# A local-attention stage with 64-key bands computed as 64x32-tile products, and value copies made by DMA

## The reference, cut to what matters

```
bk2, bv2 = (look(bk), look(bv))          # a window's own 32 keys and the 32 before
mask = (it < jb) | (it > jb + w) | (jb == -1)
sim = jnp.einsum('bhwie,bhwje->bhwij', bq, bk2) * QK_SCALE
sim = jnp.where(mask, -jnp.finfo(sim.dtype).max, sim)
attn = jax.nn.softmax(sim, -1)
out = jnp.einsum('bhwij,bhwje->bhwie', attn, bv2)
```

## Time and profile before

| | us |
|---|---|
| median of 3 runs | 2713.26 |
| lowest, highest | 2708.19, 2714.23 |
| span of the profiled execution | 2713.2 |
| one pass of the steady loop (8 slots), profiled | 38.97 to 38.99 |

### The profile page before, as it was taken

One profiled execution on the slowest core, in us unless ns is written; L12 is line 12 of the kernel. 1 busy time (PEld: TensorE's weight loads), 2 busy tenths in 40 slices (PEclk: granted clock), 3 DMA queues, 4 the chain that ended last, 5 costly groups with the idle time before them and its releaser, 6 DMA issues.

```text
span 2713.2 us, 62249 instructions
## 1 busy us (share of the span) xinstructions
PE 2525.8 (93%) x18693; PEld 2059.1 (76%) x18693; DVE 2253.2 (83%) x5097; ACT 1560.3 (58%) x3463; POOL 1737.4 (64%) x1485
## 2 busy tenths in 40 slices
PE   6999799989999899999999998999989999899998
PEld 4774577768887688886788867888768888688886
DVE  4778788878998699996899978999778989699995
ACT  3545455656665466664666655666546666466663
POOL 3444311168886487884788747887657888388883
PEclk9998899989999999999999999999999999999999
DMA  3000000100000100000000001000010000000000
GB/s 86 0 0 0 1 0 0 40 25 0 0 0 4 38 1 0 0 0 17 25 0 0 0 8 34 0 0 0 8 33 0 0 0 0 17 1 0 0 0 16
DMA packets 27720, 24.09 MB, mean 9 GB/s; under 512 B 11734, under 2 KB 24164, under 8 KB 26852
## 3 DMA queue, kind: packets, MB, share of 16 engines
q1 hardware_dynamic: 27620, 22.96, 2.9%
HBM read 21.90 MB, written 1.05 MB: 8 GB/s over the span
## 4 chain that ended last, share of the span: by engine, by line
PE 57%; DVE 17%; issue 8%; ACT 4%; DVEq 1%; POOL 1%; ACTq 0%; POOLq 0%
PE bank L688 10%; PE bank L728 7%; PE bank L754 6%; PE bank L715 5%; PE bank L493 5%; DVE l_ss L1434 4%; DVE xs_part L1411 4%; PE bank L701 4%; DVE l_rot L1424 4%; ACT l_sq L1032 3%; PE bank L742 3%; PE bank L693 3%; PE bank L645 2%; PE bank L710 2%; PE bank L634 1%
## 5 line engine op out<-in xcount | busy, mean ns | idle before, releaser
L443 POOL TENSOR_TENSOR l_rn<-l_ss,minus_half 128x8 f32<-128x8 f32 x384 | 632.3, 1647 | 192.6 <-DVE l_ss L1444 171.7
L441 POOL TENSOR_TENSOR l_qk<-l_rot 128x512 f32<-128x512 f32 x384 | 488.1, 1271 | 164.5 <-DVE l_rot L1424 162.0
L447 POOL TENSOR_TENSOR l_qk<-l_qk,l_rn 128x512 f32<-128x512 f32 x384 | 400.5, 1043 | 55.0
L1037 ACT ACTIVATE l_qkT<-bank 128x512 f32<-128x512 f32 x384 | 229.4, 597 | 334.2 <-PE bank L701 334.1
L1032 ACT ACTIVATE l_sq<-bank 128x512 f32<-128x512 f32 x384 | 229.9, 599 | 312.1 <-PE bank L688 302.5
L728 PE MATMUL bank<-l_v,probT 128*128 128x65 f32 x3072 | 389.4, 270 | 9.0 <-ACT probT L893 8.9
L728 PEld LDWEIGHTS bank<-l_v,probT 128*128 128x128 f32 x3072 | 374.8, 192 | 13.3 <-ACT probT L893 12.6
L1420 DVE TENSOR_TENSOR l_rot<-bank,l_tab 128x512 f32<-128x512 f32 x384 | 264.1, 688 | 139.6 <-ACT l_sq L1032 139.4
L1132 DVE TENSOR_REDUCE peak<-bank 128x4 f32<-128x512 f32 (+1 forms) x512 | 348.3, 680 | 36.8 <-PE bank L531 30.3
L688 PE MATMUL bank<-w_high,xs_part 128*128 128x512 f32 x768 | 341.7, 445 | 33.8 <-DVE xs_part L1411 33.8
L888 ACT ACTIVATE prob<-sm 128x512 f32<-128x512 f32 x512 | 319.1, 623 | 83.5 <-DVE sm L1140 77.3
(11 more groups left out here) (187 smaller groups left out, 4761.7 us busy)
## 6 DMA issues: line engine op xcount, KB each, us to landing
early<-in_L_ffn_Wqkv_dram SPq DMA_DIRECT2D x6, 1536.0 KB, 6.6
l_wo<-in_L_ffn_Wo_dram SPq DMA_DIRECT2D x6, 512.0 KB, 3.6
f_w<-in_L_ffn_W_dram SPq DMA_DIRECT2D x6, 341.0 KB
out_dram<-X SPq DMA_DIRECT2D x4, 256.0 KB, 2.3
f_w<-in_L_ffn_W_dram SPq DMA_DIRECT2D x6, 128.0 KB
l_oT<-in_L_xattn_Wkv_dram SPq DMA_DIRECT2D x1, 512.0 KB, 5.7
const<-in_const_dram SPq DMA_DIRECT2D x1, 392.0 KB, 3.1
f_b<-in_L_ffn_b_dram SPq DMA_DIRECT2D x24, 0.5 KB
```

Of the source, the lines that this page charges most:

```text
L441: pool.tensor_tensor(l_qk[:, k], l_rot[:, k, 0], l_rot[:, k, 1], ALU.add).then_inc(l["add_done"], 1)
L443: pool.tensor_tensor(l_rn[:, k], l_ss[:, k], minus_half[:], ALU.pow).then_inc(l["rn_done"], 1)
L447: pool.tensor_tensor(v, v, l_rn[:, k, :, None].broadcast_to([128, 8, L_DIM]), ALU.mult).then_inc(l["qk_done"], 1)
```

## The change

Every 32 queries meet the 64 keys of their band only. Scores are 16 products for a unit (2 head pairs, 4 windows, 2 halves of the rows) of 64 rows, 32 columns of queries and 64 keys, instead of four over 128 keys; the mask (l_mask) is 128 columns wide instead of 256. Peaks, subtraction, exponential and the copy of the turned probabilities take 256 columns instead of 512, and two transposes take the place of four. A turned block then holds the band keys of one head in partitions 0 to 63 and of another in 64 to 127. The products with the values are 16 of 64 rows and 32 columns, and need the values at matching partitions: besides l_v, two arrangements l_v2 (moved by 32 keys) and l_v3 (halves exchanged), which four DMAs for each batch fill on SP (move_values). They share room with buffers of the first stage (stash). PE waits for them once in a batch (moved).

The result of l_pv stands in banks 6 and 5, columns 256 on. Bank 5 also takes the turned probabilities, so l_turn waits for o_done, the divide of the unit before. The lists of stages are in another order on PE, ACT and DVE:

```diff
+BAND = 2 * WINDOW
+WINDOWS = S // WINDOW
...
+        l_mask = sb("l_mask", [128, 2 * BAND], BF16)
...
-        a_km = sb("a_km", [128, 2, 4, 128])
+        stash = sb("stash", [128, 2 * 2 * 4 * 2 * (L_DIM + 1)])
+        a_km = stash[:, 0:1024].rearrange("p (k h n) -> p k h n", k=2, h=4)
+        l_v2, l_v3 = (stash[:, 1040 * k:1040 * (k + 1)].rearrange("p (b u r n) -> p b u r n", b=2, u=4, r=2)
+                      for k in range(2))
+        a_q, a_k, a_o, a_oT = (stash[:, 1040 + 256 * k:1296 + 256 * k].rearrange("p (k n) -> p k n", k=2)
+                               for k in range(4))
...
-        l_v = sb("l_v", [128, UNROLL, 4, L_DIM + 1])
+        l_v = sb("l_v", [128, 2, 2, 4, 2, L_DIM + 1])
...
+            def move_values(ub, b, k):
+                sp.wait_ge(l["v_done"], upto(ub, 4 * b + 4))
+                apart(sp)
+                if not isinstance(b, int) or b >= 2:
+                    sp.wait_ge(l["pv_done"], upto(ub, 4 * b - 4))
+                    apart(sp)
+                for dst, half, at in ((l_v2, 0, 32), (l_v2, 1, 32), (l_v3, 0, 64), (l_v3, 1, 0)):
+                    sp.dma_start(dst[64 * half:64 * half + 64, k], l_v[at:at + 64, k, half]).then_inc(moved, 16)
+            def serve_layer(ly, last):
+                ub = ly * UNITS
+                if not last:
+                    sp.wait_ge(l["w_split"], upto(0, (ly + 1) * W_CHUNKS))
+                    apart(sp)
+                    load_projections(ly + 1)
+                for b in range(2):
+                    move_values(ub, b, b)
+                with sp.Fori(1, B // 2) as i:
+                    for k in range(2):
+                        move_values(ub, 2 * i + k, k)
+                if not last:
+                    sp.wait_ge(l["out_done"], upto(0, (ly + 1) * B))
+                    apart(sp)
+                    load_output(ly + 1)
...
+                def l_turn(u, b, j):
+                    pe.wait_ge(l["exp_done"], upto(ub, u + 1))
+                    pe.wait_ge(l["probT_done"], upto(ub, u))
+                    pe.wait_ge(l["o_done"], upto(ub, u))
+                    for r in range(2):
+                        ins = pe.transpose(bank[:, 5, r * 128:(r + 1) * 128], prob[:, j % 2, r * 128:(r + 1) * 128],
+                                           ident)
+                    ins.then_inc(l["turned"], 1)
...
-                        pe.matmul(bank[:, 3 + r, 0:256], ident_bf, mask_bf, start=True, stop=False,
+                        pe.matmul(bank[:, 3 + r, 0:2 * BAND], ident_bf, l_mask[:], start=True, stop=False,
                                   skip_group_check=True)
                     for p in range(2):
-                        for r in range(2):
-                            rows = slice(64 * r, 64 * r + 64)
-                            ins = pe.matmul(bank[:, 3 + r, 128 * p:128 * p + 128],
-                                            l_qkT[rows, j % 2, 128 * p:128 * p + 128],
-                                            l_qkT[rows, j % 2, 256 + 128 * p:384 + 128 * p],
-                                            start=False, stop=True, skip_group_check=True)
+                        for w in range(WINDOWS):
+                            keys = 256 + 128 * p + max(w - 1, 0) * WINDOW
+                            queries = 128 * p + w * WINDOW
+                            for r in range(2):
+                                rows = slice(64 * r, 64 * r + 64)
+                                ins = pe.matmul(bank[w * WINDOW:(w + 1) * WINDOW, 3 + r, BAND * p:BAND * (p + 1)],
+                                                l_qkT[rows, j % 2, queries:queries + WINDOW],
+                                                l_qkT[rows, j % 2, keys:keys + BAND],
+                                                start=False, stop=True, skip_group_check=True)
...
                 def l_pv(u, b, j):
                     pe.wait_ge(l["probT_done"], upto(ub, u + 1))
-                    pe.wait_ge(l["v_done"], upto(ub, u + 1))
                     pe.wait_ge(l["o_done"], upto(ub, u))
-                    w = L_DIM + 1
-                    for h in range(4):
-                        n = h % 2 * 2 + h // 2
-                        ins = pe.matmul(bank[:, 6, h * w:(h + 1) * w], probT[:, j % 2, n * 128:(n + 1) * 128],
-                                        l_v[:, j, h, :], start=True, stop=True)
+                    if j % 4 == 0:
+                        pe.wait_ge(moved, (ly * B + b + 1) * 64)
+                    apart(pe)
+                    k, g = j // 4, j % 4
+                    values = ((l_v[:, k, 0], l_v[:, k, 0], l_v2[:, k], l_v3[:, k]),
+                              (l_v3[:, k], l_v3[:, k], l_v2[:, k], l_v[:, k, 1]))
+                    for r in range(2):
+                        for w in range(WINDOWS):
+                            for p in range(2):
+                                rows = slice(64 * p, 64 * p + 64)
+                                at = 256 + (L_DIM + 1) * r
+                                ins = pe.matmul(bank[w * WINDOW:(w + 1) * WINDOW, 6 - p, at:at + L_DIM + 1],
+                                                probT[rows, j % 2, 128 * r + w * WINDOW:128 * r + (w + 1) * WINDOW],
+                                                values[p][w][rows, g, r], start=True, stop=True,
+                                                skip_group_check=True)
                     ins.then_inc(l["pv_done"], 1)
...
-                return Pipeline(pe, [(6, lambda u, b, j: turn(l, ub, u, j)), (4, l_scores), (7, l_turn_o), (6, l_pv),
-                                     (3, l_turn_qk), (7, l_output), (0, l_turn_x), (1, l_project)],
-                                UNITS, UNROLL, 4)
+                return Pipeline(pe, [(6, l_turn), (1, l_project), (4, l_scores), (6, l_pv), (3, l_turn_qk),
+                                     (7, l_turn_o), (7, l_output), (0, l_turn_x)], UNITS, UNROLL, 4)
...
+                def l_exp(u, b, j):
+                    act.wait_ge(l["sub_done"], upto(ub, u + 1))
+                    act.wait_ge(l["turned"], upto(ub, u - 1))
+                    act.activation(prob[:, j % 2, 0:4 * BAND], sm[:, j % 2, 0:4 * BAND], ACT.Exp, scale=QK_SCALE)\
+                       .then_inc(l["exp_done"], 1)
+                def l_copy_prob(u, b, j):
+                    act.wait_ge(l["turned"], upto(ub, u + 1))
+                    act.wait_ge(l["pv_done"], upto(ub, u - 1))
+                    act.activation(probT[:, j % 2, 0:256], bank[:, 5, 0:256], ACT.Copy).then_inc(l["probT_done"], 1)
...
-                    act.activation(l_v[:, j, :, 0:L_DIM],
-                                   bank[:, 1, 0:256].rearrange("p (h n) -> p h n", n=L_DIM), ACT.Copy)\
+                    act.activation(l_v[:, j // 4, :, j % 4, :, 0:L_DIM],
+                                   bank[:, 1, 0:256].rearrange("p (h r n) -> p h r n", h=2, r=2), ACT.Copy)\
                        .then_inc(l["v_done"], 1)
...
-                return Pipeline(act, [(6, lambda u, b, j: copy_prob(l, ub, u, j)), (1, l_copy_x),
-                                      (5, lambda u, b, j: exp(l, ub, u, j, QK_SCALE)), (7, l_copy_o), (3, l_copy_qk),
-                                      (1, l_square), (1, l_copy_v)], UNITS, UNROLL, 4)
+                return Pipeline(act, [(6, l_copy_prob), (1, l_copy_x), (5, l_exp), (1, l_square), (1, l_copy_v),
+                                      (3, l_copy_qk), (7, l_copy_o)], UNITS, UNROLL, 4)
...
                 def l_divide(u, b, j):
+                    ov = bank[:, 5:7, 256:256 + 2 * (L_DIM + 1)].rearrange("p a (r n) -> p a r n", r=2)
+                    sums = rsum[:, j % 2, 0:4].rearrange("p (a r) -> p a r", a=2)
                     dve.wait_ge(l["o_turned"], upto(ub, u - 1))
-                    invert_sums(l, ub, u, j, 4, L_DIM)
-                    divide(l, ub, u, j, 4, L_DIM, o[:, j % 2].rearrange("p (h n) -> p h n", n=L_DIM))
+                    dve.wait_ge(l["pv_done"], upto(ub, u + 1))
+                    dve.reciprocal(sums, ov[:, :, :, L_DIM]).then_inc(l["rsum_done"], 1)
+                    dve.wait_ge(l["rsum_done"], upto(ub, u + 1))
+                    dve.tensor_tensor(o[:, j % 2].rearrange("p (a r n) -> p a r n", a=2, r=2)[:, ::-1],
+                                      ov[:, :, :, 0:L_DIM],
+                                      sums[:, :, :, None].broadcast_to([128, 2, 2, L_DIM]), ALU.mult)\
+                       .then_inc(l["o_done"], 1)
...
-                return Pipeline(dve, [(0, l_copy_in), (1, l_split_x), (4, l_peaks), (2, l_floor), (4, l_shift), (6, l_divide),
-                                      (7, l_residual), (1, l_rotate), (1, l_sum_squares)], UNITS, UNROLL, 4)
+                return Pipeline(dve, [(0, l_copy_in), (1, l_split_x), (2, l_floor), (1, l_rotate), (4, l_peaks),
+                                      (4, l_shift), (1, l_sum_squares), (6, l_divide), (7, l_residual)],
+                                UNITS, UNROLL, 4)
...
```

66 lines of the change are left out of this document (40 added, 26 removed).

## The result

The changed kernel takes 3192.64 us (median; 3187.24 to 3210.04), the kernel before 2713.74 beside it: 1.177 times the time before, with an interval from 1.174 to 1.181. The forecast was 3149, with a range from 3015 to 3330.

A forecast was written before the change was run, and what follows sets the result against it. It took a circle through PE, ACT and DVE to bound the changed kernel: batch 24.32 us, 4.83 over 19.49, +406 in 84 batches; 2713 + 406 + 30 outside the loops = 3149 us, range 3015 to 3330.

The forecast's parts named there:

- The circle: Turn, project, square, rotate, peaks, shift, sum, divide, next turn lie end to end: 5.11 us a plain slot, against 4.87 average before.
- The batch's start: Slot where a batch begins: project waits for rows queued behind the probability copy, 2.19 us instead of 0.22; slot 7.08 us.
- The output slot: Slot with the output product: output waits for turn_o and copy_o; 5.06 + S+V, 7.02 us.
- S+V: PE's scores and values steps together: 64 passes at 0.0275 us plus 0.2 for the tiled shape, 1.96 us.
- the tiles really run side by side: Rival on PE's narrow products: 64 passes in 0.44 us, S+V 0.64, batch 23.0, whole 3038 us; chance 0.20.
- 25 ns floor: Skill's start-to-start floor for PE products, set against parallel tiles: S+V 1.8 us, whole 3135 us.
- The clock: Rival: PE's waits lower the granted clock, project in the circle takes 0.6 us more in 336 slots, +200, about 3350; chance 0.06.
- Outside the loops: Per layer, three more slots with turn and project (+1.2 each) and five finishing slots (+0.3 each): 5 us, +30 in six layers.
- so I cost them at nothing: Four value-copy DMAs per batch, 532 KB: about two slots (10 us) of cover before pv, so no cost.
- the circle does not bind: Rival: l_turn goes ahead of DVE's end and PE bounds; 3.8 us a slot, 2354 us; chance 0.04.

The follow-up runs named there:

- e1: Changed kernel with project ahead of the turn on PE, and copy_x and square ahead of the probability copy on ACT: 2850.35 us, 1.050 of the kernel before.
- e4: Changed kernel's tiles, masks, value moves and wait for the divide, with the PE, ACT and DVE lists of the kernel before: 2628.39 us, 0.969 of the kernel before.
- e7: Changed kernel with PE's and ACT's lists of the kernel before, DVE's list as changed: 4347.16 us, 1.602 of the kernel before.
- e6: Changed kernel with DVE's list alone taken back to the kernel before, divide ahead of rotate: 3245.32 us, 1.196 of the kernel before.
- e10: Changed kernel plus 20 unread mask products ahead of project's wait for its rows where a batch begins: 3154.59 us, 1.163 of the kernel before.
- e12: Changed kernel with the 32 narrow score products of a unit issued twice: 3292.08 us, 1.215 of the kernel before.
- e8: Changed kernel plus unread mask products, 12 ahead of the turn's wait and 20 ahead of project's at a batch's start: 3279.93 us, 1.209 of the kernel before.

## Why the prediction was right, and where two errors cancelled

**The circle.** Right, link by link: 5.18 us against 5.11, and e1, e4 and e7 move the slot in the direction that it says. e6 shows that the working named only one of the circles that crossed lists can close.

**The batch's start.** Right: 7.14 and 7.19 us in the 10 of 72 slots at the upper clock, forecast 7.08, with project waiting for the rows behind the probability copy.

**The output slot.** The mechanism was right (5.06 + S+V, output waiting for l_oT), the term S+V mis-sized: I took half of 0.055 us for a pass and 1.96 for both steps, by the width of the columns, and measured 0.79. With that the formula gives 5.85; the slots at the upper clock are 5.92 and 5.86. So the rival "the tiles really run side by side" holds: the 32 score passes start 6 to 7 ns apart and lie in 0.24 us from the first start to the last. The 25 ns floor of the Trainium skill (TensorE: Matmul & The Clock Gate, Part 1), from which the prediction had an estimate of 1.8 for S+V, isn't borne out here for tiles of 64x32. The rule of the Trainium skill (TensorEngine Tiling (Array Packing), Key Properties) that tiles load weights and multiply in parallel is. The error made a pass 2.26 us too long.

**The clock.** Not in the main case, priced as a rival at +200 us. It fell, to 0.879, but not in every slot: project ran at the lower level in 62 of the 72 slots where a batch begins, after its wait of some 1.7 us; in 20 of the 72 slots 0 and 4, whose turn waits 2.03 us; in 4 of the output slots, whose turn waits 0.95; and in none of the slots 3 and 7, whose turn doesn't wait. By the two middle rows of the table it costs 1.21 us a pass, 51 us in 42; e10 gives 38 back. The prediction's +200 took every slot's project at the lower level. The two slots 0 and 4, plain but for the turn of x, were 0.49 and 0.12 over the forecast for a plain slot; slot 0 is the first after the loop's branch.

**The sum of a pass.** 48.64 as forecast; less 2.26 for S+V; plus 0.17 for the batch's starts, 0.75 for the plain slots and 1.21 for the clock; that is 48.51, as measured. The forecast of the pass is right to 0.3% by luck: an overrated term and omitted ones nearly cancel. With S+V at 0.79 and the rest as it was, the forecast would have been 46.3 a pass and 3051 in all, near the rival's 3038 and 142 under what was measured.

**Outside the loops.** +30 us forecast, some +67 measured. The slots there cost what was said: 90.3 us for the stretch without the projection load against 83.9, 6.4 for a layer where I had 5. What the step "so I cost them at nothing" missed is the start of a layer: two slots of cover are there too, but the moves stand in SP's queue behind twelve or thirteen other issues, and in four layers they land in 7.2 to 8.6 us beside the projection load instead of in 2.4 (30.6 us in five waits). The row that priced them, 3.6 us for 512 KB, had no such load beside it. The 42 passes cost 411 us more, forecast 406; in the first pass of four layers there is a stop of PE at the layer's branch of 3.8 to 5.1 us, which before had in two (4.8 and 3.3).

**The gain that wasn't looked at.** The rival "the circle does not bind" was priced at 3.8 us a slot and 2354 us. e4, where it doesn't, has 4.52 and 2628: in its plain slots POOL's rows were the next bound (4.17). They are busy 31.46 us a pass in the earlier trace rows, 3.93 a slot, above the 3.8 that I took. I had left them out.

## What to carry to other kernels

When in-order queues are reordered, write each new list beside the lists of the engines that it exchanges buffers with, and look for every pair of steps that stands one way on one engine and the other way on the other; each such pair, together with a wait on a single buffer, can close a circle, and here the longest circle was the slot, whatever the busy shares said. Change what the tiles are and the order of the lists in separate runs: here the first brought 3% and the second cost 21%. Before adding a DMA behind a loop's weight loads, look at the place where the loop is entered, not only at its steady part: at what stands ahead in the queue and at what large load is in flight.

## What the runs showed of the hardware

- Products of 64x32 tiles, each with its own weight load, start 6 to 7 ns apart in the first 32, with longer gaps at every eighth (34, 10 and 10 ns, medians of 384 groups). With 64 in a row (e12) the last 32 start mostly 5 to 17 ns apart, 13 on average, and the whole group takes 0.64 us from first start to last instead of 0.24.
- PE's loop body has some 1350 records of products and weight loads in the changed kernel, 1430 in e10, and 1620 and 1860 in e8 and e12. The former two pass the loop's branch in 0.21 us, the latter two in 3.3 to 3.9 us in five layers and 3.8 to 4.7 in the last. The queue that loads instructions shows it; its row (packets, MB, share) of the changed kernel and then of e12:

```profile
q8 instruction: 91, 1.49, 0.2%
```

```profile
q8 instruction: 436, 7.14, 0.9%
```

- A move of 130 KB inside SBUF lands in 2.4 us in the median of the whole kernel, and in 7.2 to 8.6 us when it is issued 0.5 to 2.7 us behind a load of 1.5 MB on the same queue.
